# Rebuilding the load, the first layer norm and the attention bias of a four-layer image kernel

## What is computed

```
x = _layernorm(pair, gamma, beta)            # over the 64 channels of each place
q = (x @ Wq).reshape(B, L, L, N_HEAD, D_HID) * SCALING
...
bias = x @ Wb                                # 64 channels -> 4 heads, for each place (j, k)
gate = jax.nn.sigmoid(x @ Wg + bg)
attn = jnp.einsum('bijhd,bikhd->bijkh', q, k)
attn = attn + bias[:, None]                  # the same for every i
attn = jax.nn.softmax(attn, axis=-2)
```

## Time and profile before

| what | us |
|---|---|
| median of 3 runs | 1241.21 (1240.40 to 1241.44) |
| the profiled execution's own time | 1242.17 |
| its span, first to last instruction | 1240.4 |
| load, up to the last statistics | 0 to 55.2 |
| group norm | to 58.5 |
| norm, up to the last issue of a bias DMA | 58.5 to 155.0 |
| start of the attention, up to VectorE's first step on scores | to 162.5 |

### The profile page before, as it was taken

The page is one execution under the profiler, slowest core; times in us unless marked ns, Lnnn a source line. Parts: engine busy times, 40 slices in busy tenths (PEclk is TensorE's granted clock), DMA queues, the critical chain, the costliest instruction groups (busy, mean ns, idle before and its releaser), DMA issues. The chain is left out here.

```text
span 1240.4 us, 25484 instructions
## 1 busy us (share of the span) xinstructions
PE 1098.8 (89%) x9447; PEld 770.5 (62%) x9447; DVE 728.6 (59%) x3560; ACT 569.3 (46%) x1161; POOL 325.6 (26%) x466
## 2 busy tenths in 40 slices
PE   3677289999999969994999999999999999999688
PEld 2422067777777743443777677677777767776476
DVE  2521057787877752224566766766676677667235
ACT  1299556767676631002444444444444444443200
POOL 0100046656565631000112212221221122122111
PEclk9987679999999988995999999999999999999869
DMA  8000000000000000000000000000000000000002
GB/s 156 1 0 4 4 4 3 2 3 2 3 2 3 3 1 1 1 0 9 2 1 1 1 2 1 1 2 1 1 2 1 1 1 1 1 1 1 1 29 112
DMA packets 11487, 11.35 MB, mean 9 GB/s; under 512 B 4324, under 2 KB 9188, under 8 KB 11364
## 3 DMA queue, kind: packets, MB, share of 16 engines
q1 hardware_dynamic: 9266, 9.08, 2.9%
q10 hardware_dynamic: 2098, 0.65, 0.3%
HBM read 5.14 MB, written 4.23 MB: 8 GB/s over the span
## 5 line engine op out<-in xcount | busy, mean ns | idle before, releaser
L1460 PE MATMUL quad<-theta,nat 128*128 128x512 f32 x512 | 240.7, 593 | 0.0
L639 POOL TENSOR_TENSOR nat<-nat,arena 128x512 f32<-128x512 f32 x128 | 132.9, 1050 | 111.4 <-DVE arena L703 111.4
L1259 POOL TENSOR_TENSOR nat<-nat,const 128x512 f32<-128x512 f32 x32 | 40.6, 1268 | 439.4 <-DVE nat L1398 439.4
L1468 PEld LDWEIGHTS quad<-flat 128*128 128x128 f32 x768 | 104.6, 190 | 46.5 <-ACT flat L1290 25.1
L1468 PE MATMUL quad<-flat 128*128 128x128 f32 x768 | 123.8, 284 | 2.8 <-ACT flat L1290 1.7
L1460 PEld LDWEIGHTS quad<-theta,nat 128*128 128x128 f32 x512 | 87.5, 191 | 61.7 <-issue 61.7
L703 DVE CUSTOM_DVE_ANT_0 nat<-quad,arena 128x128 f32<-128x128 f32 x512 | 113.2, 283 | 9.7 <-PE quad L789 9.7
L1290 ACT ACTIVATE flat<-quad 128x256 f32<-128x256 f32 x192 | 73.4, 382 | 70.4 <-PE quad L1468 56.6
L662 ACT ACTIVATE nat<-bank 128x512 f32<-128x512 f32 x128 | 69.5, 595 | 57.2 <-PE bank L797 57.2
L1367 DVE SCALAR_TENSOR_TENSOR flat<-nat,c,duo 128x128 f32<-128x128 f32 x64 | 22.0, 345 | 102.0 <-PE duo L1477 102.0
L667 ACT ACTIVATE nat<-nat 128x512 f32<-128x512 f32 x128 | 77.2, 633 | 5.6 <-POOL nat L639 5.5
(11 more groups left out here) (384 smaller groups left out, 2316.2 us busy)
## 6 DMA issues: line engine op xcount, KB each, us to landing
out<-nat SPq DMA_DIRECT2D x16, 256.0 KB, 2.0
arena<-flat SPq DMA_DIRECT2D x64, 4.0 KB
const<-in_constants ACTq DMA_DIRECT2D x1, 400.5 KB, 3.2
arena<-in_L_conv_Ws SPq DMA_DIRECT2D x1, 240.0 KB
flat<-arena SPq DMA_DIRECT2D x3, 32.0 KB, 4.3
nat<-in_x SPq DMA_DIRECT2D x4, 0.2 KB, 13.0
arena<-in_L_conv_Wq ACTq DMA_DIRECT2D x1, 32.0 KB, 7.8
arena<-in_L_conv_Wk ACTq DMA_DIRECT2D x1, 32.0 KB, 7.7
```

The lines of the kernel that those rows point to most:

```text
L639: pool.tensor_tensor(scored, scored, of_head(least[b], h).broadcast_to([128, ROWS, L]), ALU.subtract).then_inc(lowered, 1)
L1259: pool.tensor_tensor(quarters(rem), quarters(rem), ident.unsqueeze(1).broadcast_to([128, ROWS, 128]), ALU.add).then_inc(diag_added, 1)
L1460: return pe.matmul(m.quad[:, n, :], vT[:, col(n)], m.theta[:, part, :], start=(part == 0), stop=False, skip_group_check=True)
L1468: last = pe.matmul(m.quad[:, row, place * C:(place + 2) * C], a8[g % 2][:, col(row)], zs[half][k % 2][:, n, :], start=False, stop=(k == 2) ...
```

## The change

**Load.** The two loads that the powers need (alpha, theta) are issued first on ScalarE's queue and have a semaphore of their own; Wo is loaded here too; layer 1's ten loads go to SP's queue behind `x`. TensorE turns four banks before anything else, the alpha chain comes first on VectorE and the weights are folded after the first doubling. Four doublings remain (powers up to 16), and the turns of the image are spread between them. GpSimd fills `pick` here, VectorE halves Wo here.

**Norm.** TensorE makes powers 17 to 32 with two 512-column products at the start and ScalarE copies them; `theta` waits for them. VectorE now adds the shift into `z` straight from PSUM and squares it (`keep_centre`, two steps a bank in place of one), ScalarE has only Ln and Exp: Ln for banks 0 to 5, Exp for those six, then five and five again. One over the deviation of all 16 banks is kept in `nat`. GpSimd scales banks 0 to 10 of `z`, VectorE banks 11 to 15, after its last square. The bias is made with 128 places of `z` as the stationary operand and `w0b`, now 8 columns wide, as the moving one: 64 small products into one PSUM bank, 24 of them between banks 12 to 15 and 40 at the end.

**Attention.** VectorE adds the heads' constants from that bank, TensorE turns the four heads by transposes, VectorE copies the result to `m.bias`. There is no bias DMA. At the very end of layer 3 a semaphore is used again in place of a new one.

```diff
-    DOUBLINGS = [1, 2, 4, 8, 16]
+    DOUBLINGS = [1, 2, 4, 8]
+    TURNED_FIRST = 4
+    TURNED_BY = [4, 6, 8, 10]
+    MEASURED_BY = [4, 4, 5, 7]
...
             act.dma_start(m.const[:, :], args["constants"]).then_inc(consts_in, 16)
+            for dst, src in early:
+                act.dma_start(dst, src).then_inc(early_in, 16)
             for dst, src in vectors:
                 act.dma_start(dst, src).then_inc(weights_in, 16)
-            for dst, src in loads1:
-                act.dma_start(dst, src).then_inc(S("l1_loaded"), 16)
-            act.wait_ge(weights_in, 16 * len(vectors))
+            act.wait_ge(early_in, 16 * len(early))
...
+    LAG = 2
+    BATCH_ENDS = (6, 11, BANKS)
+    POOL_SCALES = BATCH_ENDS[1]
+    BIAS_AFTER = {LAG + 10: (0, 2), LAG + 11: (2, 4), LAG + 12: (4, 6), LAG + 15: (6, BANKS)}
...
+            for q in range(POOL_SCALES):
+                pool.wait_ge(rstd_ready, q + 1)
+                pool.wait_ge(squared, q + 1)
+                pool.tensor_tensor(m.z[:, cols(q)], m.z[:, cols(q)], rstd(q), ALU.mult).then_inc(z_ready, 1)
...
+            for p in range(BANKS):
+                act.wait_ge(var_made, p + 1)
+                act.activation(rstd(p), var_bank[p], ACT.Ln, bias=m.eps[:, :]).then_inc(logged, 1)
+                if p + 1 in BATCH_ENDS:
                     act.wait_ge(logged, p + 1)
+                    for n in range(done, p + 1):
+                        act.activation(rstd(n), rstd(n), ACT.Exp, scale=-0.5).then_inc(rstd_ready, 1)
+                    done = p + 1
...
+            for at in range(2):
+                pe.matmul(m.quad[:, 2 + at, :], m.power_turn, m.pw[0:C, 1 + 8 * at:9 + 8 * at, :], start=True, stop=True).then_inc(last_made, 1)
...
+                    for pair in range(4 * bank, 4 * bank + 4):
+                        last = pe.matmul(m.quad[:, 2, pair * 8:(pair + 1) * 8], m.z[:, pair * L:(pair + 1) * L], m.w0b[:, :],
+                                         start=True, stop=True)
...
+            def keep_centre(q):
+                dve.wait_ge(centred, q + 1)
+                dve.tensor_scalar(m.z[:, cols(q)], m.bank[q % 4][:, :], centre_shift, None, ALU.add).then_inc(centre_kept, 1)
+                dve.wait_ge(centre_kept, q + 1)
+                if q >= 4:
+                    dve.wait_ge(var_made, q - 3)
+                dve.tensor_tensor(squares[q % 4], m.z[:, cols(q)], m.z[:, cols(q)], ALU.mult).then_inc(squared, 1)
...
-            dve.wait_ge(m.sem("bias_laid"), 16 * 64)
+            dve.wait_ge(m.sem("z_bias_made"), 1)
+            dve.tensor_tensor(by_head(bias_turned), by_head(m.quad[:, 2, :]), m.head_bias[:, :].unsqueeze(1).broadcast_to([128, L, HEADS]),
+                              ALU.add).then_inc(bias_kept, 1)
...
+            for h in range(HEADS):
+                last = pe.transpose(turn_a[:, row(h)], bias_turned[:, h:HEADS * L:HEADS], ident)
```

More of the change, by code:

```diff
@@ L284, in _ @@
             step(dve.tensor_scalar(powers[:, 1:2], alpha[:, 5:6], H_STEP, None, ALU.mult))
+            dve.tensor_scalar(theta_raw, theta_raw, H_STEP, None, ALU.mult)
+            step(dve.tensor_scalar(turn[:, C:2 * C], ident64, powers[0:C, 1:2], None, ALU.mult))
+            step(dve.tensor_tensor(turn[:, 0:C], theta_raw, turn[:, C:2 * C], ALU.subtract))
+            dve.tensor_copy(turn[:, C:2 * C], turn[:, 0:C]).then_inc(S("a_turn"), 1)
             have = 2
@@ L438, in layer0_norm @@
     spread, centre_shift = m.take(128), m.take(1)
-    squares = [m.take(CH) for _ in range(2)]
-    logs, rstd = ([m.nat[:, (4 * n + b) * CH:(4 * n + b + 1) * CH] for b in range(4)] for n in range(2))
+    squares = [m.take(CH) for _ in range(4)]
+    m.bias_turned = m.take(CH)
     S = lambda name: m.sem(f"z_{name}")
@@ L532, in _, with scale @@
         def _(dve):
+            step = m.chain(dve, "dve")
+            def keep_centre(q):
[5 more added lines that the diff above has]
+                dve.tensor_tensor(squares[q % 4], m.z[:, cols(q)], m.z[:, cols(q)], ALU.mult).then_inc(squared, 1)
+            def scale(first, end):
+                for q in range(first, end):
+                    dve.wait_ge(rstd_ready, q + 1)
+                    dve.wait_ge(squared, q + 1)
+                    dve.tensor_tensor(m.z[:, cols(q)], m.z[:, cols(q)], rstd(q), ALU.mult).then_inc(late_z_ready, 1)
             dve.tensor_scalar(spread, away, m.scale2[:, :], None, ALU.mult).then_inc(spread_ready, 1)
             dve.wait_ge(shift_made, 1)
-            dve.tensor_copy(centre_shift, m.quad[:, 3, 0:1]).then_inc(shift_ready, 1)
+            dve.tensor_copy(centre_shift, m.bank[3][:, 0:1]).then_inc(shift_ready, 1)
             dve.wait_ge(shift_ready, 1)
-            step = m.chain(dve, "dve")
+            keep_centre(0)
+            keep_centre(1)
             dve.wait_ge(S("early_turned"), 1)
@@ L542, in _ @@
                               m.turned1[0:C, 256:256 + TAPS].unsqueeze(2).broadcast_to([C, TAPS, C]), ALU.mult).then_inc(S("early_spread"), 1)
+            for q in range(2, 6):
+                keep_centre(q)
             dve.wait_ge(S("early_taps"), 1)
@@ L580, in layer0_attention @@
     factor, gated = m.take(CH), m.take(CH)
-    wo = m.take(C)
+    wo, pick = m.wo, m.pick
+    bias_turned = m.take(CH)
     least = [m.take(HEADS * ROWS) for _ in range(2)]
-    pick = m.take(HEADS * 32).rearrange("p (h d) -> p h d", h=HEADS)
     sums = m.take(128)
@@ L628, in _ @@
             step = m.chain(pool, "pool")
-            step(pool.memset(pick, 0.0))
-            for h in range(HEADS):
-                step(pool.memset(pick[:, h, h:h + 1], 1.0))
-            pool.sem_inc(pick_ready, 1)
             for g in range(STEPS0):
@@ L813, in add_up @@
                 last.then_inc(sums_made, 1)
-            pe.wait_ge(pick_ready, 1)
             project_qk(0)
-            pe.wait_ge(S("wo_halved"), 1)
+            pe.wait_ge(bias_kept, 1)
+            for h in range(HEADS):
+                last = pe.transpose(turn_a[:, row(h)], bias_turned[:, h:HEADS * L:HEADS], ident)
+            last.then_inc(bias_made, 1)
             for g in range(STEPS0):
```

287 lines of the change are left out of this document (137 added, 150 removed).

## The result

| what | before | after |
|---|---|---|
| median, us | 1241.18 | 1188.64 (1187.14 to 1189.75) |
| ratio to before, 95% interval | | 0.957 [0.956, 0.959] |
| profiled execution, and its span | 1242.17, 1240.4 | 1187.14, 1185.3 |
| last statistics of the load | 55.2 | 42.2 |
| norm, first product to the end | 96.5 (58.5 to 155.0) | 57.0 (45.6 to 102.6) |

The forecast was 1189.5. The span is 55.1 us shorter, which is more than the 52.5 of the medians: the profiled execution is the fastest of the four after, and was 1.0 us above its median before. Of the 55.1, 12.9 are the load, 39.5 the norm, 1.4 the attention's start and 1.3 lie behind it.

A forecast was written before the change was run, and what follows sets the result against it. The prediction took ScalarE's table loads to bound the norm, with TensorE the bound afterwards. Load 12.4, norm 38.1 and attention's start 1.2 sum to 51.7 us off the median 1241.21: 1189.5 us, range 1182 to 1203.

The forecast's parts named there:

- The bound: Norm: ScalarE, over half its work table loads, binds it before; afterwards ScalarE is off the path and TensorE binds.
- the rival with the 26 loads back: Norm: the 26 other table loads come back, ScalarE needs 63 us and binds again, about +10, 1200; chance 0.01.
- Load, -12.4: Load: the last statistics end at 42.8 us in place of 55.17, 12.4 us less.
- The late-landing rival: Load: alpha and theta land at 16.4 as before, the load ends 5.3 us later, 1194.8; chance 0.09.
- Norm, -38.1: Norm: the stage takes 58.4 us on TensorE in place of 96.5, 38.1 us less.
- narrow products at full clock: Norm: 64 products with 8 moving columns at 0.243 us each, 15.5 us, all on TensorE's path.
- the slower case: Norm: loading 128 x 128 stationary operands costs much more; loses from 1.05 us a product, 1251 at 1.2; chance 0.02.
- waits: Norm: TensorE waits 0.8 us for VectorE at bank 2's average and 1.9 for a PSUM bank at bank 9's, sum 2.8.
- Clock in the tail, 4.0: Norm's end: the clock falls about halfway through the 40 narrow products, 17 x (0.47 - 0.243) = 4.0 us.
- The port, 1.3 us: Norm: VectorE's squares and GpSimd's scalings exclude each other at SBUF's port, 1.3 us in sum, held by the waits.
- Attention's start, -1.2: Attention's start: the projection comes 0.45 us after the norm, where it was 1.7 after SP's last issue; 1.2 us less.
- First step on scores: Attention's start: VectorE's first step on scores at 110 to 111 us, as a sign that the forecast is right.

The follow-up runs named there:

- the wide kernel: The changed kernel with 128 moving columns (120 of them zeros) in place of 8 for the 40 narrow products at the norm's end: 1183.3 us, ratio 0.953.
- the combined kernel: The changed kernel with both power products moved to the load's end and 128 moving columns for the tail's 40 products: 1177.9 us, ratio 0.949.

## Why the prediction was right, step by step

- **The bound.** Right: ScalarE off the path (16.4 us idle ahead of Ln), TensorE busy 96% of the norm. Putting the table loads back filled ScalarE again, but the rival with the 26 loads back was priced at about +10, 1200, and +17.6 was measured, 1206.6. Its 63 us of ScalarE were right (63.4 in the trace), but the list's gapless part of 61.8 us begins only 10.7 us into the norm, and 4.2 us follow it.
- **Load, -12.4.** Measured -12.9. VectorE's first step at 13.20 (forecast 13.1), the weights' products done at 21.79 (22.5), the last statistics at 42.24 (42.8). The late-landing rival is real at +5.1 and didn't happen.
- **Norm, -38.1.** Measured -39.5, by terms: the start with two centrings 7.5 us (8.0); banks from start to start 0.86 (0.86); narrow products at full clock 0.231 (0.243, from the row with one row stationary; the full 128 rows cost no more, so the slower case was empty); waits 0.8 for VectorE and 1.4 for the PSUM bank at bank 9 (0.8 and 1.9, 2.2 for 2.8 in sum). That the 0.8 agrees is luck: it was forecast for the average of bank 2, which waits 0.26, and 0.49 of it is at bank 0, for the square that stood beside `theta`.
- **Clock in the tail, 4.0** (17 x 0.227 is 3.9). Measured 13.33 - 40 x 0.231 = 4.1. That it would fall in the tail was reasoned from the earlier trace rows; where was a guess, and the close agreement is luck in part: by the same working the tail lost 3.3 us with the power products moved and 6.8 with `theta` behind the scalings. The two parts of it were each a little off: 18 products at full and 22 at the low clock (23 and 17 forecast), but 9.22 / 22 = 0.42 us each there and not 0.47. The 1.42 / 3 counts the end of the last product in. The next product of the kernel before starts 20.88 - 19.60 = 1.28 us behind the first of the three, which is 0.43 each:

```profile
20.88 0.56 PE L354 MATMUL quad<-arena 64*128 64x1 f32 x2
```

The row of layer 3, with 1.2 GHz at full busy share, was the right one to go by; that of layer 1, 1.94 us long, was not. The Trainium skill, "TensorE: Matmul & The Clock Gate", Part 1, states that the clock is set by how busy the engine has lately been, and that a busy one has the full clock; by that rule the tail would have been 9.2 us. The trace does not agree: busy 9.21 of 9.22 us at 0.50, and in the wide kernel the clock stays at 1.00 once the same products move more columns.
- **The port, 1.3 us.** This step was wrong in its mechanism, though it changed nothing in the sum, where the waits held it: the scalings cost the norm nothing, and the only wait by the port was 0.5 us at the first square, through `theta`. I counted each square's delay as if TensorE stood right behind it; it is two banks behind (LAG = 2). The Trainium skill, "SBUF — State Buffer", "Who interferes with whom", states that a VectorE instruction with two SBUF inputs contends with a GpSimd instruction that reads SBUF. The trace agrees: squares of 0.69 us alone take up to 2.27 beside GpSimd. Whether that costs the kernel time is another question.
- **Attention's start, -1.2.** Measured -1.4: the projection 0.32 behind the norm, 5.79 us to the first step (5.8). The 5.8 was taken over from the kernel before, where this stretch stood at 0.50 too, and I did not ask for its clock; here it stays at 0.50 behind the narrow tail. At the full clock it is 3.93 us.
- **First step on scores** at 108.75, forecast 110 to 111: the load (0.5) and the norm (1.4) were both forecast too long. Behind it the span is 1.3 us shorter, which wasn't foreseen and is within what this part varies by (see the last section).
- **What was weighed and missing.** The forecast counted the power products as moved from one path to another, 3.75 us for nothing. It did not ask whether TensorE had idle time beside the last statistics: it had about 2 us, and there the granted clock was 1.00.

## What to carry to other kernels

Where a chain of table functions binds ScalarE, count its table loads first; but half of them gone gave only 14 of 20.5 us in the kernel before, where PSUM buffers and DMAs held up the rest, so follow what each later engine waits for. When a matrix engine runs many small products with a fresh stationary operand each, look at the granted clock of that stretch and of the one behind it, and try wider moving operands, with zeros if need be: here they were free and gave 6 us. Put work of the matrix engine that has no urgency into the stretch ahead of a stage's end in which it idles, and not at the head of the next stage: here the same two products took 1.99 us in the one place, at 1.00, and 3.77 in the other, at 0.50.

## What the hardware showed that was not expected

- A float32 product with 128 x 128 places stationary takes 0.227 us with 128 moving columns and 0.231 with 8, at the full clock; at the low clock 0.42 with 8.
- The same unedited instructions behind the attention's start took 1074.1 to 1077.9 us in different kernels (1078.6 in one more, the combined kernel with `theta` moved), and the unedited load ended at 41.8 to 43.8 us (the one with the power products at 40.7 in one kernel and at 43.8 in another). A single trace can therefore be 3 to 4 us off in its span, and stages are to be compared by their own start. What differs in the load was not followed up and stays open.
- VectorE's square and GpSimd's product lengthen each other: beside scalings 0.69 became 0.98 to 1.72 us, and GpSimd's scalings took 1.26 to 1.72, 1.71 in the median, where the mean in the earlier trace rows is 1.27.
